# Linear attention times gated experts: other places for the exponentials, a third buffer for key/value sums, stores on other queues

## The reference

```python
xn = _layernorm(x)                                   # x: 4 x 1024 x 1024
q, k, v = xn @ Wq.T + bq, xn @ Wk.T + bk, xn @ Wv.T + bv
kv_sum = cumsum((elu(k) + 1) * v, axis=1)            # along the sequence
s = ((elu(q) + 1) * kv_sum * 64 ** -0.5) @ Wo.T + bo
probs = softmax(xn @ router_w.T); top_p, top_i = top_k(probs, 2)
# slots: 8 experts x 256 rows, filled in order of choice, later ones dropped
h = gelu(buf @ w1.T + b1, approximate=False) @ w2.T + b2
g = silu(sum over a token's kept slots of h * top_p)
out = x + s * g
```

## Time and profile before

| | |
|---|---|
| median of 3 runs | 2158.04 us (2155.92 to 2165.63) |
| the profiled execution, its time and its span | 2165.84 us, 2163.7 us |
| TensorE busy | 2002.2 us, 93% of the span |
| VectorE, ScalarE, GpSimd busy | 1372.5, 688.0, 469.4 us |
| mean granted clock of TensorE | 0.969 of full speed |
| DMA traffic | 419.87 MB, mean 194 GB/s |

### The profile page before, as it was taken

One profiled execution on the slowest core, in us unless ns is written; L12 is line 12 of the kernel. 1 busy time (PEld: TensorE's weight loads), 2 busy tenths in 40 slices (PEclk: granted clock), 3 DMA queues, 4 the chain that ended last, 5 costly groups with the idle time before them and its releaser, 6 DMA issues. The chain is left out here.

```text
span 2163.7 us, 27040 instructions
## 1 busy us (share of the span) xinstructions
PE 2002.2 (93%) x9380; PEld 911.0 (42%) x9380; DVE 1372.5 (63%) x2074; ACT 688.0 (32%) x1087; POOL 469.4 (22%) x569
## 2 busy tenths in 40 slices
PE   7799999998868898999999999879999999999993
PEld 2245544544323343444444444334444444444441
DVE  3677877887576667677767776465544554455453
ACT  1322222222452524443444343332222222222221
POOL 0078888888515000000000000110000000000002
PEclk9899999999888999999999999989999999999996
DMA  8667666766995776766676667963343333333334
GB/s 291 216 203 232 234 213 223 246 215 200 324 342 149 262 243 210 262 218 227 220 264 210 238 211 245 288 161 127 104 170 106 102 103 97 107 101 98 104 117 78
DMA packets 183606, 419.87 MB, mean 194 GB/s; under 512 B 17808, under 2 KB 77264, under 8 KB 181712
## 3 DMA queue, kind: packets, MB, share of 16 engines
q1 hardware_dynamic: 144784, 297.90, 42.1%
q0 software_dynamic: 26848, 109.12, 15.9%
q10 hardware_dynamic: 11872, 11.54, 1.8%
HBM read 268.51 MB, written 166.77 MB: 201 GB/s over the span
## 5 line engine op out<-in xcount | busy, mean ns | idle before, releaser
L1739 PE MATMUL pair<-arena 128*128 128x512 f16 x3360 | 733.2, 380 | 17.5 <-DVE arena L1421 11.3
L1701 PE MATMUL pair<-xnT,arena 128*128 128x512 f16 x2400 | 542.4, 386 | 58.4 <-ACT arena L905 33.8
L1739 PEld LDWEIGHTS pair<-arena 128*128 128x128 f16 x3360 | 329.4, 98 | 418.4 <-issue 25.7
L1426 DVE SCALAR_TENSOR_TENSOR arena<-pair,arena 128x1024 f32<-128x1024 f32 x248 | 303.0, 1223 | 191.1 <-PE pair L1739 190.7
L1623 PE MATMUL pair<-arena 128*128 128x512 f16 x1728 | 385.2, 381 | 7.8 <-DVE xnT L419 7.8
L1701 PEld LDWEIGHTS pair<-xnT,arena 128*128 128x128 f16 x2400 | 236.5, 99 | 357.1 <-ACT arena L905 36.7
L923 ACT ACTIVATE arena<-arena 128x512 f16<-128x512 f32 x280 | 170.2, 626 | 606.6 <-PE pair L1739 524.5
L1623 PEld LDWEIGHTS pair<-arena 128*128 128x128 f16 x1728 | 169.3, 98 | 203.3 <-issue 13.5
L1701 PE MATMUL pair<-xnT 128*128 128x512 f16 x960 | 214.1, 379 | 0.0
L1402 DVE SCALAR_TENSOR_TENSOR arena<-arena 128x512 f16<-128x512 f32 x280 | 188.9, 684 | 13.2 <-ACT arena L923 11.2
L743 POOL DMA_INDIRECT out<-xnT,meta_s x8 | 13.9, 1735 | 708.7 <-DVE xnT L1434 706.5
(11 more groups left out here) (188 smaller groups left out, 1740.8 us busy)
## 6 DMA issues: line engine op xcount, KB each, us to landing
down_dram<-arena SPq DMA_DIRECT2D x70, 512.0 KB, 4.0
arena<-down_dram SPq DMA_DIRECT2D x70, 512.0 KB, 3.3
up_dram<-arena SPq DMA_DIRECT2D x100, 256.0 KB, 3.7
arena<-up_dram SPq DMA_DIRECT2D x100, 256.0 KB, 2.6
arena<-w_up POOLq DMA_DIRECT2D x40, 512.0 KB, 5.4
up_sums<-arena POOLq DMA_DIRECT2D x40, 512.0 KB, 3.7
arena<-w_down POOLq DMA_DIRECT2D x40, 512.0 KB, 5.5
down_sums<-arena POOLq DMA_DIRECT2D x40, 512.0 KB, 3.4
```

Of the source, the lines that this page charges most:

```text
L1426: ins = nc.vector.scalar_tensor_tensor(to, src, scale, to, ALU.mult, ALU.add)
L1701: ins = mm(out_to, w[:, a, c * P:(c + 1) * P], x_in_op[:, b, c, :], start=(first and i == 0), stop=(i == 11), skip_group_check=True)
L1739: ins = mm(bank[2 + h][:, (t % 2) * BLOCK:(t % 2 + 1) * BLOCK], g_ops[:, A_NAMES.index(name), c, a, t * P:(t + 1) * P], down_ring[:, j, c, ...
```

## The change

The exponentials of an attention quad go to the places of S2 and S1 in turn, not to `copy_a`; the copies lose their waits for `phi_ready`, and the exponential waits for the low half of the S2 or S1 that last used the place, or for the context two before. `keep_p16` stands ahead of value 0 in these quads, value 3 and context 3 ahead of the high and low half of "12". `kvq` gets a third buffer, over `logits` and `small` (now parts of one tensor `routing`), and slices are loaded two contexts ahead, the first three of each half before its first quad. The gate weights are made during the sums of x. The six stores of x are issued by SyncE, ahead of everything else there, and the first four up loads after `sums_stored`. The first down operands wait for the stored weight sums only from j = 4 on. `save_s` moves to GpSimd's queue.

```diff
         HOLE = BLOCK // 2
+        KQ = 3
         kvq = [xnT_rows[:, 8 + 2 * u:10 + 2 * u, HOLE:2 * HOLE] for u in range(2)]
...
+        routing = sb("routing", [P, 2 * TILES * EXPERTS + 2 * TOPK * TILES], F32)
+        logits = routing[:, 0:TILES * EXPERTS].rearrange("p (t e) -> p t e", e=EXPERTS)
+        small = routing[:, TILES * EXPERTS:2 * TILES * EXPERTS].rearrange("p (n t) -> p n t", t=TILES)
+        keep, prob = (routing[:, 2 * TILES * EXPERTS + u * TOPK * TILES:2 * TILES * EXPERTS + (u + 1) * TOPK * TILES]
+                      .rearrange("p (k t) -> p k t", k=TOPK) for u in range(2))
+        kvq.append(routing[:, 0:BLOCK].rearrange("p (r s) -> p r s", r=2))
...
-            def save_s(n):
-                half = n // GROUPS
-                for c, added in ((C11, 4), (C12, 10), (C22, 12), (C21, 14)):
-                    sp.wait_ge(down_added, 14 * n + added)
-                    tile = HALF_TILES * half + PAIRS * (c // 2)
-                    e = slice((c % 2) * BLOCK, (c % 2 + 1) * BLOCK)
-                    sp.dma_start(s_dram[tile:tile + PAIRS, :, e].rearrange("t p e -> p t e"), acc[:, :, c, :])\
-                      .then_inc(s_stored, 16)
...
             sp.wait_ge(sums_done, 1)
-            for a in range(US):
-                load_up_op(a)
+            for name in ("11", "21", "22"):
+                c, s = X_AT[name]
+                for h in (HI, LO):
+                    sp.dma_start(xop_dram[X_NAMES.index(name), :, h], xnT[:, h, c:c + 4, s + 2 * BLOCK:s + 3 * BLOCK])\
+                      .then_inc(xraw_saved, 16)
...
             sp.wait_ge(tail_stored, 16 * tails + 16)
             sp.nop().then_inc(sums_stored, 1)
+            for a in range(US):
+                load_up_op(a)
...
                 if n == 0:
                     sp.wait_ge(down_added, 10)
                     load_row(b_2)
-                if n == ATT_GROUPS - 1:
-                    save_s(n)
...
             for n in range(8):
+                if n == ATT_GROUPS - 1:
+                    save_s(n)
...
             for half in range(HALVES):
+                if half:
+                    save_s(GROUPS + ATT_GROUPS - 1)
                 for i in range(HALF_TILES):
                     add_rows(half, i)
...
                 if n:
                     act.wait_ge(down_done, 28 * (n - 1) + 4 * j + 4)
                     act.wait_ge(down_saved[j], 16 * n)
-                elif j == 0:
-                    act.wait_ge(sums_stored, 1)
+                elif j == 4:
...
                     stored(act, len(UNITS))
...
             def keep_p1(k):
                 if k:
                     act.wait_ge(quad_sum, 4 * (k - 1) + 3)
-                    if is_attention((k - 1) // 2):
-                        act.wait_ge(phi_ready, 4 * attention_quad(k - 1) + 4)
...
             def keep_p165(k):
                 act.wait_ge(quad_sum, 4 * k + 1)
-                if is_attention(k // 2):
-                    act.wait_ge(phi_ready, 4 * attention_quad(k) + 1)
                 keep_product(k, 2, copy_a, UP.index(5))
...
+            KVQS = [(k, i) for k in range(QUADS) if is_attention(k // 2) for i in range(4)]
+            KVQ_HALF = len(KVQS) // HALVES
...
+            def load_kvq(a):
+                k, i = KVQS[a]
+                if a >= KQ:
+                    act.wait_ge(ctx_ready, a - KQ + 1)
                 name = VALUES[i]
-                act.dma_start(kvq[a % 2], kvs_dram[f_chunk(k, name), :, slots(k, name)]
-                              .rearrange("p (r s) -> p r s", r=2)).then_inc(kvq_loaded[a % 2], 16)
+                act.dma_start(kvq[a % KQ], kvs_dram[f_chunk(k, name), :, slots(k, name)]
+                              .rearrange("p (r s) -> p r s", r=2)).then_inc(kvq_loaded[a % KQ], 16)
...
                 col = f_chunk(k, name)
                 if is_attention(k // 2):
                     a = 4 * attention_quad(k) + i
-                    if i == 0:
-                        load_kvq(k, 0)
-                        load_kvq(k, 1)
-                    elif name == "22":
-                        act.wait_ge(quad_sum, 4 * k + 3)
-                    if i:
-                        act.wait_ge(phi_ready, a)
-                    nc.scalar.activation(copy_a, in_rows(src), ACT.Exp, bias=bq_c[:, col:col + 1], scale=INV_XM)
+                    to = ("S2", "S1")[i % 2]
+                    if i < 2:
+                        if k:
+                            act.wait_ge(g_lo, made_count(k - 1, to))
+                    else:
+                        act.wait_ge(phi_ready, a - 1)
+                    nc.scalar.activation(g_block(to), src, ACT.Exp, bias=bq_c[:, col:col + 1], scale=INV_XM)
                     nc.scalar.activation(g_block(name), src, ACT.Relu, bias=bq_c[:, col:col + 1], scale=INV_XM)\
                       .then_inc(hidden, 1)
-                    if i in (1, 2):
-                        load_kvq(k, i + 1)
+                    ahead = a + KQ - 1
+                    if a % KVQ_HALF and ahead // KVQ_HALF == a // KVQ_HALF:
+                        load_kvq(ahead)
...
-            act.wait_ge(xsum_done, 1)
-            for name in ("11", "21", "22"):
-                c, s = X_AT[name]
-                for h in (HI, LO):
-                    act.dma_start(xop_dram[X_NAMES.index(name), :, h], xnT[:, h, c:c + 4, s + 2 * BLOCK:s + 3 * BLOCK])\
-                       .then_inc(xraw_saved, 16)
-            for i in range(16):
-                high_x_sum(i)
-            act.wait_ge(xraw_saved, 96)
-            for i in range(16, 32):
-                high_x_sum(i)
-                if i >= 20 and i % 2 == 0 and i < 30:
-                    high_up(0, (i - 20) // 2)
-            act.wait_ge(xsum_done, 32)
-            for j in (5, 6):
-                high_up(0, j)
             def gate_weights():
                 act.wait_ge(scaled, 1)
...
+            for i in range(16):
+                high_x_sum(i)
+                if i == 1:
+                    gate_weights()
+            act.wait_ge(xraw_saved, 96)
+            for i in range(16, 32):
+                high_x_sum(i)
+                if i == 23:
+                    act.wait_ge(sums_stored, 1)
+                    act.wait_ge(xsum_done, 24)
+                    load_kvq(0)
+                    load_kvq(1)
+                    act.wait_ge(meta_ready, 1)
+                    load_kvq(2)
+                if i >= 20 and i % 2 == 0 and i < 30:
+                    high_up(0, (i - 20) // 2)
+            act.wait_ge(xsum_done, 32)
+            for j in (5, 6):
+                high_up(0, j)
...
+                late = is_attention(k // 2)
+                if late:
+                    keep_p16(k)
                 value(k, 0)
                 if ups:
                     high_up(k + 1, 1)
-                keep_p16(k)
+                if not late:
+                    keep_p16(k)
...
                     high_up(k + 1, 5)
+                if late:
+                    value(k, 3)
                 if in_line(k):
                     high_g(k, "12")
-                value(k, 3)
+                if not late:
+                    value(k, 3)
...
                 if last:
+                    if half == 0:
+                        for a in range(KQ):
+                            load_kvq(KVQ_HALF + a)
...
-            for i in range(32):
-                low_x_sum(i)
-                if i >= 20 and i % 2 == 0 and i < 30:
-                    low_up(0, (i - 20) // 2)
-            for j in (5, 6):
-                low_up(0, j)
+            nc.vector.tensor_tensor(prob[:, :, :], prob[:, :, :],
+                                    rstd_t[:, 0:TILES].unsqueeze(1).to_broadcast((P, TOPK, TILES)), ALU.mult)
+            nc.vector.tensor_tensor(logits[:, :, :], logits[:, :, :],
+                                    rstd_t[:, 0:TILES].unsqueeze(2).to_broadcast((P, TILES, EXPERTS)), ALU.mult)\
+              .then_inc(scaled, 1)
...
+            for i in range(32):
+                low_x_sum(i)
+                if i == 3:
+                    gate_weights()
+                if i >= 20 and i % 2 == 0 and i < 30:
+                    low_up(0, (i - 20) // 2)
+            for j in (5, 6):
+                low_up(0, j)
...
                 a = 4 * attention_quad(k) + i
                 v = g_block(VALUES[i])
                 dve.wait_ge(hidden, 4 * k + i + 1)
-                nc.vector.scalar_tensor_tensor(in_rows(v), copy_a, 1.0, in_rows(v), ALU.min, ALU.add).then_inc(phi_ready, 1)
+                nc.vector.scalar_tensor_tensor(v, g_block(("S2", "S1")[i % 2]), 1.0, v, ALU.min, ALU.add).then_inc(phi_ready, 1)
                 dve.wait_ge(phi_ready, a + 1)
-                dve.wait_ge(kvq_loaded[a % 2], 16 * (a // 2 + 1))
-                nc.vector.scalar_tensor_tensor(in_halves(v), in_halves(v), SCALE, kvq[a % 2],
+                dve.wait_ge(kvq_loaded[a % KQ], 16 * (a // KQ + 1))
+                nc.vector.scalar_tensor_tensor(in_halves(v), in_halves(v), SCALE, kvq[a % KQ],
```

(2 more changed lines are left out.)

37 lines of the change are left out of this document (13 added, 24 removed).

## The result

The kernel after takes 2148.0 us (median of six runs, 2145.1 to 2152.8) where the kernel before, run beside it, takes 2162.3 (six runs): ratio 0.9939, interval 0.992 to 0.9959. It is faster by 0.6%, where 2.5% was forecast, and outside the range. On two later occasions the same kernel took 2134.1 us beside 2165.6 (0.9848, interval 0.9823 to 0.9873) and 2132.4 beside 2163.5 (0.986, 0.9832 to 0.9888), so the first comparison holds a loss of some 14 us that doesn't always come. Both later medians lie just above the range's upper end of 2131. I call each such group of runs on one chip a session; there were six.

A forecast was written before the change was run, and what follows sets the result against it. TensorE, busy 2002.2 of 2163.7 us, was taken as the bound, leaving its idle time and low clock to win. Terms -1 + 21 + 4 + 11 + 18 + 2.5, less 1, took 54.5 off 2158.0: 2104 us, range 2082 to 2131.

The forecast's parts named there:

- d: First three quads and first output product: late loads and sums come sooner, 21 us gained; bounds 8 and 26.
- Part b: Third slice buffer ends the second half's 3.63 us wait; gate weights move into the operand sums, at most 3 us.
- c: Six x stores issued from SyncE: the first up operand is late instead, 1 us lost; bounds 15 lost, 4 won.
- e: Quads 3 and 4: the 2.46 us wait goes, 2.98 shrinks to 1.4; 4 us gained, bounds 0 and 7.
- f: First output's stores on GpSimd's queue: up operand no longer queued behind them, 11 us gained; bounds 5 and 13.
- No wait over 3 us near 808: Sign of being right in the profile after, where TensorE's 10.49 us wait in quads 3 and 4 stood.
- g: Second half, quads 20 to 22: product 1 of the next quads starts sooner, 18 us gained; bounds 12 and 27.
- the second "wrong" sign: VectorE still waits for slices of the key/value sums in the profile after.
- Part a: Exponentials in the places of S2 and S1, new order: quad 23's 1.82 us wait goes, 1.4 stays per first-half quad.
- the first rival: DMA engines bound the front and loads land as now: 24 us less gain, 2128 us; chance 0.22.
- The other rivals: Nearly everything goes, 2080 us (chance 0.08); no effect, 2155 (0.03); slower through a late start, 2169 (0.03).

The follow-up runs named there:

- experiment 8: After with its 32 scatters issued a second time in a quiet stretch of the second half: 2134.2 us beside after's 2134.1.
- experiment 9: After again, 2132.4 us; after with scatters held until quad 2 ended, 2125.2; before with only the exponentials' places and order changed, two buffers, 2165.1.
- experiment 1: After with GpSimd's 32 table scatters held until quad 2 has ended on TensorE: 2141.7 us, ratio 0.9896.
- experiment 5: After with scatters spread, eight ahead of each x copy in steps 3 to 6: 2135.2 us; also with first up loads ahead of the x stores: 2129.3.
- experiment 3: Before with the gate weights alone moved into the operand sums, so the scatters start earlier: 2172.5 us, ratio 1.0048.
- Experiment 6: Before with its scatters alone spread, eight ahead of each x copy in steps 3 to 6: 2163.3 us, ratio 1.0016.
- Loads first: First four up loads issued ahead of the six x stores: on after 2142.7 us, on after with scatters spread 2129.3 us.
- experiment 2: After with SyncE's first four up loads issued ahead of the six x stores: 2142.7 us, ratio 0.9894.
- experiment 4: Before with the stores of the attention output alone on GpSimd's queue: 2161.4 and 2157.7 us; after with that move undone: 2138.7 us.

## Why the prediction was wrong

**Where it failed: d, and the sentence on the scatters.** Part b says that they "move ahead too. Nothing waits for them until the first half's end", and the sum gives them and the gate weights 1 us. No instruction waits for them, but the transfers beside them take longer: 12 to 13 us more of all 16 DMA engines (experiment 8), and the change puts them under quads 0 and 1, where the share was 0.89. The cleanest comparison is the one-line edit in session 5, with no unexplained wait in either kernel: d's piece is 119.3 us with the scatters there and 102.5 without (experiment 9). Experiments 1 and 5 say the same, and experiment 3 (9 to 10 us by themselves) too, though with a wait of the first two sessions in it. Against before's 127.5 us, d's piece without them is 24 to 25 shorter, more than the forecast 21; with them it is 9 shorter in the later sessions and 1.5 in the first. With them gone from both kernels it is 117.7 before and 103.3 after, so 14 us is what the rest of the change gives.

The same step had a wrong reading in it. The 6.35 us for which VectorE stood for a slice was put down to the slice's place in the order. Experiment 6 shows that it was mostly the scatters beside it, which the third buffer doesn't cure.

**c** was -1 and measured -4.3 to -6. The operand-sum copies did start 2 us after the first sum, as forecast, and the six stores took 7.0 us to issue. What failed is "I leave it there" for the tail store. The window store, now behind the six stores, went out 9.0 us after the first operand sum instead of 3.4, and the tail store, which waits for it, another 19.7 us later (18.8 before). Taking off the 7.2 us by which this profile's operand sums began late, the tail store stands at 569.6 where the forecast left it at 563.0, and the first up load at 574.1 where its terms give 569. ScalarE had the operand 4.0 us after that issue, as forecast, and TensorE's first up product came 5.5 us later, against the forecast 5.3. In the profiles of sessions 4 and 5 the load went out 2.6 and 4.9 us later than forecast and took 6.7 and 5.2. Loads first shortens this piece by 3 us (experiments 2 and 5), but mostly doesn't keep it.

**e and f** together were 15 and measured 10 to 12. "No wait over 3 us near 808" held: 2.49. For f the section of the Trainium skill that the prediction weighed ("Issuing engines are not separate DMA queues", DMA: Bandwidth & Descriptors) left 2 us. The medians say 2.5 to 6 and the wait itself 8.7 to 10.5, so more than that was won; my 11 was still too high.

**g** was 18 and measured 11 to 15. Its first half, product 1 of quad 21, came to within 0.1 us, and experiment 9 shows that the order alone has nearly all of that half. The second half failed as the second "wrong" sign says: a slice still late beside the accumulating transfers. The third buffer is what keeps the gain; the order alone is worth nothing in time (experiment 9). The third buffer with the old order wasn't run. Part a's use of quad 23 as "the order alone" held in part where no load is late (the last piece, 2.1 for 2.5, of which experiment 9's kernel, without the buffer, has 1.3).

**The rivals.** The bound at the front is the DMA engines, as the first rival says, and its 2128 us lies nearer to the later sessions than 2104. Its reason is not what was found: it held the bytes to be the limit, and with the scatters away the same window carries more (364 GB/s at a share of 0.98 from 592 to 640 us, where after's third profile has 236 at 1.00) and d comes down by 24 us. The other rivals did not come.

**What stays open.** In sessions 1 and 2 every kernel with scatters moved (after, experiments 1, 2 and 3) had waits of 5.7 to 19.1 us without a named end on ScalarE or VectorE while they ran; before and experiment 4 had none beside them, and in sessions 3 to 6 no kernel had one, after and experiment 1's kernel among them. It isn't the chip alone: sessions 2 and 6 ran on the same one. Nor need it be the session: experiment 2's two pairs of timings, 13 us apart, would fit waits that come and go from one execution to the next, but each kernel has one profile a session. Two instruction packets of that moment in after took 2138 and 718 ns instead of about 950 and 309, which would fit an engine short of its own instructions. But experiments 2 and 3 had such waits without such packets, and session 5's after had a packet of 1366 ns instead of 309 without such a wait. What differs between the sessions I don't know. After's median differs by 14 us, 2148 and 2134; how much of that is these waits isn't shown either, since in the profiles only 7 to 8 us of the difference lie in d's piece and 6 to 7 ahead of any scatter.

## What to carry to other kernels

When an edit moves small indirect transfers, price them by what they add to the DMA engines' busy time and not by their bytes or by who waits for them. Put them where nothing beside them is urgent: they cost nothing at a DMA share of 0.3, and 5 us a group or next to nothing at 0.6 to 0.8. A wait for a DMA names the victim: look at what else was on the engines before blaming its place in the order. And run the unchanged kernel again beside any experiment that gains more than its edit can explain.

## What was not expected of the hardware

- 30 scatters of 128 rows of 8 bytes add 12 to 13 us of busy time on all 16 DMA engines, almost none of it in their own packets, and make loads of 256 KB take 6.8 instead of 2.5 us, at a share of 0.64; at the front, 18.7 (session 5) instead of 7.5 (session 3).
- The same six stores of 512 KB take 15.2 us to issue from ScalarE and 7.0 from SyncE.
- One program's median differs by 14 us between sessions in which the kernel before differs by 3, and by 12 and 13 us between two pairs of timings of one session (experiment 2).
